# Two network layers on one core: the second attention's projection as three float32r products of split operands, with four edits beside it

## The reference

```python
xn = layernorm(x, ln_x_g, ln_x_b)            # x: the 77 context rows
ln = layernorm(latents, ln_l_g, ln_l_b)      # latents: the 1024 tokens of a batch
q = ln @ Wq.T
kv = jnp.concatenate([xn @ Wkv.T, ln @ Wlkv.T], axis=1)
k, v = (kv[..., :INNER], kv[..., INNER:])
qn = rmsnorm(q, qn_g) * SCALE                # four heads of 64
kn = rmsnorm(k, kn_g)
attn = softmax(einsum('bhid,bhjd->bhij', qn, kn))
out = attn @ v; return out @ Wo.T + bo
```

## Time and profile before

| | |
|---|---|
| median of three runs | 923.14 us (922.33, 924.48, 923.14) |
| profiled execution | 925.02 us, its span 923.3 us |
| mean granted TensorE clock | 0.978 |
| TensorE busy | 877.1 us, 95% |
| VectorE busy | 632.3 us, 68% |
| ScalarE busy | 526.8 us, 57% |
| GpSimd busy | 400.1 us, 43% |

### The profile page before, as it was taken

How to read it: one execution, slowest core, us unless ns; L and a number is a source line. 1 busy time by engine, 2 the same in 40 slices (tenths; PEclk the granted TensorE clock), 3 DMA queues, 4 the chain that set the end, 5 groups by cost and what they waited for, 6 DMA issues and landing times.

```text
span 923.3 us, 15247 instructions
## 1 busy us (share of the span) xinstructions
PE 877.1 (95%) x4335; PEld 628.3 (68%) x4336; DVE 632.3 (68%) x1386; ACT 526.8 (57%) x834; POOL 400.1 (43%) x397
## 2 busy tenths in 40 slices
PE   8989989999999999999989999999999999999991
PEld 4646655545556656655557887878888888888881
DVE  6787968866567557656677789746666666666666
ACT  2567865546665775775545434326666666666650
...
GB/s 296 104 0 1 1 1 1 1 4 347 190 284 331 226 271 366 221 234 396 201 220 222 52 1 1 12 335 325 316 36 34 80 346 340 206 96 246 119 5 183
DMA packets 49776, 153.58 MB, mean 166 GB/s; under 512 B 6255, under 2 KB 24427, under 8 KB 44101
## 3 DMA queue, kind: packets, MB, share of 16 engines
...
## 4 chain that ended last, share of the span: by engine, by line
PE 68%; DVE 13%; DMA 6%; ACT 4%; POOL 4%; issue 3%; SPq 1%; DVEq 0%; ACTq 0%; POOLq 0%
PE banks L1092 10%; PE banks L1343 8%; PE banks L1345 8%; PE banks L1344 8%; PE banks L1060 3%; PE banks L1084 3%; PE banks L1085 3%; DMA wsplit<-cv_hl 2%; PE banks L994 2%; PE banks L1381 2%; PE banks L1380 2%; PE banks L1382 2%; PE banks L1356 2%; POOL cv_hl L701 2%; DMA ring<-wsplit 2%
## 5 line engine op out<-in xcount | busy, mean ns | idle before, releaser
L1092 PE MATMUL banks<-wexp 128*65 128x512 f32 (+1 forms) x288 | 149.8, 601 | 2.5 <-ACT wexp L1654 2.5
L701 POOL TENSOR_TENSOR cv_hl<-wexp,cv_hl 128x1024 fp32r<-128x1024 f32 x45 | 108.7, 2422 | 51.7 <-ACT cv_hl L1631 51.1
L1343 PE MATMUL banks<-ring,x_hi 128*128 x312 | 127.4, 408 | 0.0
L1345 PE MATMUL banks<-ring,x_lo 128*128 x312 | 122.0, 391 | 0.0
L1344 PE MATMUL banks<-ring,x_hi 128*128 x312 | 121.8, 390 | 0.0
L1654 ACT ACTIVATE wexp<-banks 128x512 f32<-128x512 f32 x128 | 75.9, 597 | 47.6 <-PE banks L1085 47.5
L1790 ACT ACTIVATE banks<-wexp 128x1024 f32 x72 | 73.5, 1020 | 47.7 <-DVE aux L2550 47.7
L1768 ACT ACTIVATE aux<-banks 128x512 f32<-128x512 f32 x78 | 46.6, 598 | 61.2 <-PE banks L1345 45.3
L1084 PE MATMUL banks<-q_hi,k_hl 128*128 128x512 f32 x144 | 77.2, 536 | 1.7 <-ACT q_lo L1622 1.0
L2148 DVE TENSOR_REDUCE neg_ab<-banks 128x1 bf16<-128x736 f32 x64 | 59.3, 927 | 23.7 <-PE banks L1060 20.1
L1345 PEld LDWEIGHTS banks<-ring,x_lo 128*128 128x128 f32 x312 | 58.6, 188 | 13.1
...
...
...
## 6 DMA issues: line engine op xcount, KB each, us to landing
...
```

The costliest lines, as they stand in the source:

```text
L701: g.tensor_tensor(sides(hl[:, PIECE:2 * PIECE]), raw, sides(hl[:, 0:PIECE]).bitcast(f32), ALU.subtract).then_inc(s['cv_lo'], 1)
L1092: mm(pb[5 + half][0:DA, :], vh[b][0:w, c, :], pT[q % 3][0:w, :], start=c == 0, stop=c == len(KTILES) - 1).then_inc(s['a_pv'], 1)
L1343: mm(o[:], x_hi[u][:, kc, :], hi, start=kc == 0 and not primed, stop=False, skip_group_check=primed)
L1345: last = mm(o[:], x_lo[u][:, kc, :], hi, start=False, stop=primed and kc == KC - 1, skip_group_check=primed)
```

## The change

**Projection.** The weights are split once: `w_hi` is `wT` rounded to float32r by ScalarE in the preparation (`weights_hi`, one copy of 128x1536), `w_lo` is the rest, by VectorE (`weights_low`, one subtraction, ahead of `ternary`). For each tile VectorE applies gain and bias to the two transposes (`proj_full`), ScalarE rounds the result (`proj_T`, now one copy of 128x256), VectorE subtracts (`proj_low`), and TensorE makes twelve float32r matmuls in place of the four float32 ones. VectorE makes tile t + 2 in its turn t.

**Order on VectorE in the projection.** Sums of squares stand one tile behind. The inverse roots of tiles 8 to 15 are made with a square root by ScalarE (`root(LN_EARLY, T)` behind `proj_kept(3)`, with the table load `ready(Sqrt)` moved there) and six small operations (`norm`) at t = 4. k of head 0 is scaled at t = 9 instead of t = 8. Head 0's first five splits stand together at t = 11.

**Feed-forward net.** The eight `bn_stats` of tiles 8 to 15 are divided into 2, 2 and 4 behind turns -3, -2 and -1. The first two `proj_tokens` stand inside turn T - 4. GpSimd's chains of inverse roots lie between its tiles, and two of its memsets per head buffer move to the program's start. TensorE's bias step of the last tile moves between the transposes of tiles 0 and 1.

**End of the attention.** The j = 1 halves of the shared weights are loaded first, on a semaphore of their own, and `up(0, 0)` waits for the j = 0 halves (`ld_sh1`) only when it comes to them. `CONV_END` moves three late conversion pieces one step earlier.

Some semaphores are merged (`ld_b1` and `ld_bias_f` into `ld_rows`, `f_add` into `y_add`).

```diff
-            for a in (0, 2 * I2, WEXP, WEXP + 2 * I2):
-                load(ring[:, a:a + 2 * I2].bitcast(f32), wsplit[0][:, a:a + 2 * I2], 'ld_sh')
+            for a, to in ((2 * I2, 'ld_sh'), (WEXP + 2 * I2, 'ld_sh'), (0, 'ld_sh1'), (WEXP, 'ld_sh1')):
+                load(ring[:, a:a + 2 * I2].bitcast(f32), wsplit[0][:, a:a + 2 * I2], to)
...
             def proj_in(t):
                 pe.wait_ge(s['l_xh'], t + 1)
                 if t > 0:
-                    pe.wait_ge(s['l_xT'], t)
+                    pe.wait_ge(s['l_xT'], t + 1)
                 for kc in range(KC):
...
                 if k == 0:
-                    pe.wait_ge(s['l_xT'], t + 1)
+                    pe.wait_ge(s['l_xT'], t + 2)
+                    if t == 0:
+                        pe.wait_ge(s['l_xlo'], 1)
                     if t >= 2:
                         pe.wait_ge(s['l_qk'], t - 1)
                 a, n = ((0, 2 * D), (2 * D, D))[k]
+                o, at = pb[PROJ_BANK[t % 2] + k][:, 0:n], slice(t % 4 * P, (t % 4 + 1) * P)
                 for kc in range(KC):
-                    last = mm(pb[PROJ_BANK[t % 2] + k][:, 0:n], xnT[:, kc, t % 4 * P:(t % 4 + 1) * P], wT[:, kc, a:a + n], start=kc == 0, stop=kc == KC - 1)
+                    mm(o, xT_hi[:, kc, at], w_hi[:, kc, a:a + n], start=kc == 0, stop=False)
+                for kc in range(KC):
+                    mm(o, xT_hi[:, kc, at], w_lo[:, kc, a:a + n], start=False, stop=False)
+                if k == 0:
+                    pe.wait_ge(s['l_xlo'], 2 * t + 3)
+                for kc in range(KC):
+                    last = mm(o, xT_lo[:, kc, at], w_hi[:, kc, a:a + n], start=False, stop=kc == KC - 1)
                 if k:
                     last.then_inc(s['l_qkv'], 1)
...
                 if i == T - 4:
                     pe.wait_ge(s['f_rows'], T)
                     proj_in(0)
+                    ffn_bias(T - 1)
                     proj_in(1)
                     pe.wait_ge(s['f_amax'], T - 1)
...
-            for t in range(4, TB + 3):
+            for t in range(4, TB + 4):
                 proj(t)
-            for k in range(2):
-                turned(0, 0, 0, k, pb[HEAD0_BANK[k]])
-            proj(TB + 3)
-            for k in range(2, 5):
-                if k >= 3:
-                    pe.wait_ge(s['t_free'], k - 2)
+            for k in range(3):
                 turned(0, 0, 0, k, pb[HEAD0_BANK[k]])
             pe.wait_ge(s['a_const'], 1)
             for t in range(TB + 4, T):
                 proj_part(t, 0)
+                if t == TB + 4:
+                    for k in range(3, 5):
+                        pe.wait_ge(s['t_free'], k - 2)
+                        turned(0, 0, 0, k, pb[HEAD0_BANK[k]])
                 maxima(0, 0, 0, 2 * (t - TB - 4), HEAD0_MAX)
                 proj_part(t, 1)
                 if t + 2 < T:
...
                 for j in (1, 0):
+                    if ci == side == 0:
+                        pe.wait_ge(s['ld_sh' if j else 'ld_sh1'], 32)
...
             def proj_T(t):
-                act.wait_ge(s['l_xT_full'], t + 1)
+                act.wait_ge(s['l_xlo'], 2 * t + 2)
                 if t >= 4:
                     act.wait_ge(s['l_qkv'], t - 3)
-                for kc in range(KC):
-                    last = a(xnT[:, kc, t % 4 * P:(t % 4 + 1) * P], pb[7][:, kc * P:(kc + 1) * P], ACT.Identity,
-                             scale=lg[:, kc:kc + 1], bias=lb[:, kc:kc + 1])
-                last.then_inc(s['l_xT'], 1)
+                a(xT_hi[:, :, t % 4 * P:(t % 4 + 1) * P], x_full[t % 2].rearrange("p (a b) -> p a b", a=KC), ACT.Copy).then_inc(s['l_xT'], 1)
...
             for t in range(3, T):
                 proj_kept(t)
+                if t == 3:
+                    ready(ACT.Sqrt)
+                    root(LN_EARLY, T)
...
+            def proj_full(t):
+
+                ve.wait_ge(s['l_xT_full'], t + 1)
+                for kc in range(KC):
+                    last = v.tensor_scalar(x_full[t % 2][:, kc * P:(kc + 1) * P], pb[7][:, kc * P:(kc + 1) * P], lg[:, kc:kc + 1], lb[:, kc:kc + 1], ALU.mult, ALU.add)
+                last.then_inc(s['l_xlo'], 1)
+
+            def proj_low(t):
+
+                ve.wait_ge(s['l_xT'], t + 2)
+                if t >= 4:
+                    ve.wait_ge(s['l_qkv'], t - 3)
+                at = slice(t % 4 * P, (t % 4 + 1) * P)
+                v.tensor_tensor(xT_lo[:, :, at], x_full[t % 2].rearrange("p (a b) -> p a b", a=KC), xT_hi[:, :, at].bitcast(f32), ALU.subtract)\
+                    .then_inc(s['l_xlo'], 1)
...
+                if i == T - 4:
+                    ve.wait_ge(s['f_pool'], T + 1)
+                    for t in range(2):
+                        proj_tokens(t)
...
             def between(i):
+                if i == -3:
+                    attended_stats(2, 0, 2)
+                if i == -2:
+                    attended_stats(2, 2, 4)
+                if i == -1:
+                    attended_stats(3)
+                    aggregate(TB, T)
+                    v.tensor_scalar(root_a[:, TB:T], mv[:, TB:T, 1], LN_EPS, None, ALU.add).then_inc(s['f_rstd'], 1)
...
                 if i == T - 4:
-                    ve.wait_ge(s['f_pool'], T + 1)
-                    ve.wait_ge(s['f_xqT_full'], T)
-                    for t in range(4):
-                        proj_tokens(t)
-                if T - 3 < i < T:
-                    proj_tokens(i - T + 6)
+                    for t in range(2):
+                        proj_full(t)
+                        proj_tokens(t + 2)
+                        proj_low(t)
+                if T - 3 <= i < T:
+                    proj_full(i - T + 5)
+                    if i > T - 3:
+                        proj_tokens(i - T + 6)
+                    proj_low(i - T + 5)
...
             for t in range(T):
                 if t >= TB + 4:
                     maximum(0, 2 * (t - TB - 4), HEAD0_MAX)
-                    maximum(0, 2 * (t - TB - 4) + 1, HEAD0_MAX)
-                if t == T - 1:
-                    maximum_both(0)
+                if t + 4 == LN_EARLY:
+                    norm(LN_EARLY, T, 0.0, ln_r)
+                if 5 <= t + 2 < T:
+                    proj_full(t + 2)
                 if 6 <= t + 4 < T:
                     proj_tokens(t + 4)
-                proj_squares(t)
-                if t == 3:
-                    scales(LN_EARLY, T, ln_r, 1.0 + LN_EPS, LN_EPS ** 2)
+                if 5 <= t + 2 < T:
+                    proj_low(t + 2)
+                if t >= TB + 4:
+                    maximum(0, 2 * (t - TB - 4) + 1, HEAD0_MAX)
+                if t == TB:
+                    root_means(0, NSA, 0, TB)
+                    scaled(0, 0, (0,))
+                elif t > 0:
+                    proj_squares(t - 1)
+                if t in (TB - 1, T - 1):
+                    proj_squares(t)
+                if t == 1:
+                    aggregate(LN_EARLY, T)
+                    v.tensor_scalar(root_a[:, LN_EARLY:T], mv[:, LN_EARLY:T, 1], 1.0 + LN_EPS, LN_EPS ** 2, ALU.mult, ALU.add)\
+                        .then_inc(s['root_in'], 1)
                 if t == 4:
                     context_squares()
                 if t == TB - 1:
                     mean_squares(0, NSA, TB)
-                if t == TB:
-                    root_means(0, NSA, 0, TB)
-                    scaled(0, 0)
-                if t == TB + 2:
-                    for k in range(2):
+                if t == TB + 1:
+                    scaled(0, 0, (1,))
+                if t == TB + 3:
+                    for k in range(5):
                         low(0, 0, k, pb[HEAD0_BANK[k]])
-                if t == TB + 3:
-                    for k in range(2, 5):
-                        low(0, 0, k, pb[HEAD0_BANK[k]])
+                if t == T - 1:
+                    maximum_both(0)
```

104 lines of the change are left out of this document (57 added, 47 removed).

## The result

| | before | after |
|---|---|---|
| median | 923.21 us (921.27 to 924.48, 7 runs) | 925.88 us (924.83 to 927.22, 7 runs) |
| ratio | | 1.0034, 95% interval 1.0022 to 1.0046 |
| profiled execution, span | 925.02, 923.3 us | 925.86, 924.1 us |
| first squares to head 0's maxima | 48.97 us | 59.14 us |

A forecast was written before the change was run, and what follows sets the result against it. TensorE was taken to bound the kernel, VectorE the projection up to tile 11. Terms -5.2 - 2.4 + 6.0 - 2.1 = -3.7 gave 921.3 from the profiled 925.02, less 1.88 to the median: 919.4 us, range 913.0 to 925.5.

The forecast's parts named there:

- start of the feed-forward net: Divided statistics cut TensorE's 2.75 us wait to about 0.5 and its clock stays at 1.00: -5.2 us.
- its tail, without the split: End of the feed-forward net: TensorE's waits of 1.94 and 0.99 go, first projection runs at full clock: -4.3 us.
- end of the attention: With j = 1 halves loaded first, six of twelve matmuls of `up(0, 0)` run from 469.3: -2.1 us.
- new order in the projection: VectorE saves the `scales` chain and waits for squares and maxima, less replacement operations and a wait for ScalarE's root: -6.8 us.
- the split, projection and tail: Full-precision steps +4.4, low steps +4.9, hand-overs +3.5 in the projection, and +1.9 us at the feed-forward net's end.
- The 6.2 of the chain: Projection: VectorE's chain of `scales`, 149.14 to 155.32, goes: -6.2 us.
- The wait of 1.9 for the squares: Projection: VectorE's wait for GpSimd's squares goes, since they are a tile behind: -1.9 us.
- the 1.5 for the maxima: Projection: of VectorE's 2.5 us waiting for TensorE's scores, 1.5 goes.
- R1: Feed-forward net's start: the clock falls anyway, giving -1.5 instead of -5.2; 923.1 us, chance .20.
- R4: End of the attention gives nothing, as third and fourth load take the bandwidth as before; 921.5 us, chance .10.
- R3: Projection costs 12.9 through TensorE's wait before tile 11, low steps contending with GpSimd and half clock; 926.3 us, chance .13.
- R2: TensorE stays the projection's bound and VectorE has room, so it gives -8 instead of +6; 905 us, chance .07.

The follow-up runs named there:

- e5: The kernel before with the eight statistics divided 2, 2, 4 and GpSimd's inverse roots of tiles 8 to 15 moved to tiles 6 and 7; 919.81 us, 0.9947.
- e9: e3 with the projection loop in the order of before on VectorE, ScalarE and TensorE; 911.92 us, 0.9873 of before.
- e2: The kernel before with only the j = 1 halves of the shared weights loaded first, on their own semaphore; 920.76 us, 0.9975.
- e3: The changed kernel with four float32 matmuls again and no split of rows and weights, all else kept; 911.72 us, 0.9881 of before.
- a0: The changed kernel with the expert stage's semaphore targets held to at least 2; 927.80 us, 1.0064 of before.
- e12: The changed kernel, split kept, with the projection loop in the order of before; 926.38 us, 1.0039 of before.
- e1: The kernel before with only the eight statistics of tiles 8 to 15 divided 2, 2, 4; 925.88 us, 1.0023.
- c0: The kernel before with the expert stage's semaphore targets held to at least 2 by a register operation; 922.97 us, 1.0003.

## Why the prediction was wrong, step by step

The parts, in us of 923.2 by the ratios, beside the terms as the prediction put them:

| term | predicted | measured | from |
|---|---|---|---|
| start of the feed-forward net | -5.2 | -4.9 | e5 |
| its tail, without the split | -4.3 | about -4.5 | e9 less e5 less e2 |
| end of the attention | -2.1 | -2.3 | e2 |
| new order in the projection | -6.8 | about 0 (+0.7 without the split, -0.5 and +2.3 with it) | e3 less e9; after and a0 less e12 |
| the split, projection and tail | +12.8 + 1.9 = +14.7 | +15.3 | e12 less e9 |

The measured terms are differences of ratios with intervals of 1 to 2 us to either side, some across chips. By the medians the start is -2.8 and the tail -5.9, with about the same sum. The clearest check leaves the split out: my terms then give 923.1 - 5.2 - 4.3 - 2.1 = 911.5 without the new order and 904.7 with it. Measured were 911.9 (e9) and 911.7 (e3).

**The step that failed is the credit for the new order**, "-6.2 + 2.1 - 1.9 - 1.5" with the +0.7 for ScalarE's root, 6.8 us of the account of VectorE. None of it is seen in the time, and in the stretch 2.3 us without the split and under 1 with it:

- The 6.2 of the chain was its time beside GpSimd's work. Alone it takes 3.9 (e12), and its replacement takes 3.3, not 2.1. The chain, from 149.14 to 155.12 in the earlier trace rows, is fourteen small operations behind the aggregate, of which ten take 0.2 (I had counted eighteen). I read the sum and not its parts, and I charged contention to the low step alone.
- The wait of 1.9 for the squares also goes in e12, where the squares are not moved.
- Of the 1.5 for the maxima, which had waited 2.5 before, 0.4 at most is the order's (waits of 1.7 ahead of L2211 in e12 and 1.3 ahead of L2205 after).
- Without the split TensorE is busy 45.0 of 49.6 us in e9, so less than 5 us could be had at all, whatever VectorE saves. I had added up VectorE alone.

The profiles of before and after by themselves would have hidden this. Between them the chain gives 2.9, the squares 1.9 and the maxima 1.2, together 6.0 of the 6.8. Only e12, with the split and without the order, shows that the order is not what brought them.

**The split** came out near its sum in the time, by errors that cancel. In the stretch alone it costs 9.5 (e12 less e9) to 11.9 us (after less e3) instead of 12.8. The full-precision step was .64 a pair from start to start, not .40: the row that I took for it, a cast of 4x128 from PSUM (.20 from start to start), was no measure for this operation of 128x128 (.32), and the 22 cost 7.0 us, not 4.4. The low step came to 6.8 us busy, some 5.9 with its overlap, not 4.9. The hand-overs were cheaper: 1.8 us in all ahead of the low step instead of 3.5. I took .45 for the low step because GpSimd's work "does not always read", but its squares and sums there all read SBUF. In the tail the split costs 2.9 (feed-forward net's last transposes to the first squares, 18.0 us in e9 and 20.9 in e12) instead of 1.9. Stretch and tail make 12.4 of e12's 15.3; its profile begins the feed-forward net 2.6 us later than e9's, with a clock of 0.83 from 20 to 30 us, which the changed kernel's does not show, so some of the 15.3 may be chance. The bounds of my sum were added wrongly too: by its own terms they are +1.3 and +11.0, not +3.5 and +10.4. The stretch grew by 10.2.

**The start** was right in mechanism: the clock was 1.00 from 64 to 76. Rival R1 fell here. But e1 shows a dependence that I had not named: the division alone loses. I had taken GpSimd's move as a matter of its own list. And the size was read in one profile whose clock was lower than others': the 0.50 from 64.45 to 76.50 was 0.75 in c0 and 0.72 in e2 with the same code, and their feed-forward nets are 2.4 us shorter.

**The tail** was right without the split: waits of 1.94 and 0.99 with the half clock behind them, -4.3, and 22.3 us from the last transposes to the first squares before against 18.0 in e9.

**The end** was right, and R4 fell. The loads came in 4.9 to 11.0 us here, so `up(0, 0)` did not wait at its seventh matmul at all.

**The rivals.** R3 was the nearest in time (926.3), and it named GpSimd's contention and TensorE's waits, but its mechanism is half right. TensorE did fall to half clock in the projection. By a0 against the changed kernel that cost 0.3 us at most. VectorE itself is the price. Its 12.9 also leaves out its own wait of 3.5 (6.0 + 4.2 + 2.7). R2 fell: TensorE is busy 44.80 of 59.14 us.

**The comparison.** My sum of -3.7 stood against a profiled execution of 925.02 that was itself 1.8 above the median of its kernel. In the pair of profiles the change is +0.84, in the medians +2.67. Of the 6.5 us between forecast and result (925.88 - 919.4) about 2 come from this: I read the start's gain in that profile, lower clock and all, and then took 1.88 off for its distance from the median as well. The other 4.5 are the miss between the profiles, and 4.2 of them lie in the stretch (10.2 instead of 6.0). There the failed credit is larger than the miss, since the split cost less than I had put it at.

**The better kernel.** e3 and e9, the change without its main part, run in 911.7 and 911.9 us, 1.2% below before.
